# Cross attention: where SP issues the store of a batch's normalised rows

## What is computed

```python
def _L1_xattn_ref(q, k, v, gamma):              # q = x, k = v = ctx_2048: (8, 256, 512)
    qh = q.reshape(B, 8, 32, 512)               # 8 heads of 32 of the 256 rows
    ...
    qk = jnp.einsum('bhdq,bhdl->bhql', qh, kh) * scale
    sm = jax.nn.softmax(qk, axis=-1)            # over the 512 columns of the context
    ret = jnp.einsum('bhql,bhdl->bhdq', sm, vh)
    return gamma * ret.reshape(B, 256, 512)

x = _layernorm(x + _L1_attn_ref(x, ...))
x = _layernorm(x + _L1_xattn_ref(x, ctx_2048, ctx_2048, gamma))    # this stage
x = _layernorm(x + _L1_ffn_ref(x, ...))                            # experts
return x
```

## Time and profile before

| | us |
|---|---|
| median of 3 runs | 1998.21 |
| the runs | 2000.76, 1998.21, 1996.4 |
| the profiled execution | 2000.18 |
| its span, first to last instruction | 1998.4 |
| mean granted TensorE clock (share of full) | 0.965 |
| PE / DVE / ACT / POOL busy | 1812.1 / 1244.1 / 930.9 / 299.9 |

### The profile page before, as it was taken

One profiled execution on the slowest core, in us unless ns is written; L12 is line 12 of the kernel. 1 busy time (PEld: TensorE's weight loads), 2 busy tenths in 40 slices (PEclk: granted clock), 3 DMA queues, 4 the chain that ended last, 5 costly groups with the idle time before them and its releaser, 6 DMA issues. The chain is left out here.

```text
span 1998.4 us, 33002 instructions
## 1 busy us (share of the span) xinstructions
PE 1812.1 (91%) x12272; PEld 1488.5 (74%) x12272; DVE 1244.1 (62%) x2286; ACT 930.9 (47%) x2388; POOL 299.9 (15%) x377
## 2 busy tenths in 40 slices
PE   7999999999996999999999996799997698888985
PEld 6889999998984878888888885677775455555554
DVE  4654444444438655555554526788887588778866
ACT  2333333333334433333333213667667488887843
POOL 0000000000012111111111001333334212112012
PEclk9999999999998999999999997999997799999998
DMA  4310000000024221101110013001002576564612
GB/s 161 110 60 1 22 22 22 22 22 22 1 66 120 86 73 43 48 27 34 46 37 17 11 43 126 11 31 35 33 22 82 151 182 146 134 162 112 157 43 84
DMA packets 83581, 131.42 MB, mean 66 GB/s; under 512 B 9344, under 2 KB 25344, under 8 KB 83424
## 3 DMA queue, kind: packets, MB, share of 16 engines
q1 hardware_dynamic: 83424, 129.33, 22.7%
HBM read 75.21 MB, written 20.53 MB: 48 GB/s over the span
## 5 line engine op out<-in xcount | busy, mean ns | idle before, releaser
L2262 ACT ACTIVATE e_p<-e_s_ps,e_nb 128x512 f32<-128x512 f32 x256 | 175.6, 702 | 45.6 <-DVE e_nb L2326 43.5
L2326 DVE TENSOR_REDUCE e_nb<-e_s_ps 128x2 f32<-128x1024 f32 x128 | 155.8, 1217 | 50.6 <-PE e_s_ps L2421 49.6
L1703 ACT ACTIVATE p<-p,nb,rq 128x128 f32<-128x128 f32 (+1 forms) x256 | 136.9, 541 | 93.2 <-DVE nb L1804 93.2
L2431 PE MATMUL e_t_ps<-ident,e_p 128*128 128x128 f32 x1024 | 147.9, 284 | 22.0 <-DVE e_pT L2333 13.4
L2431 PEld LDWEIGHTS e_t_ps<-ident,e_p 128*128 128x128 f32 x1024 | 120.8, 146 | 59.2 <-issue 50.7
L887 PE MATMUL yp<-ccy,toep 128*128 128x288 f32 x600 | 158.9, 412 | 5.8 <-ACT ccy L869 4.0
L1224 DVE SCALAR_TENSOR_TENSOR hm<-gu_ps,us_col,sg 128x256 f32<-128x256 f32 x88 | 42.3, 480 | 177.7 <-ACT sg L1113 177.7
L80 PE MATMUL q_ps<-a_xt_hi,wq_hi 128*128 128x256 f32 x512 | 149.8, 293 | 0.0
L82 PE MATMUL q_ps<-a_xt_hi,wq_lo 128*128 128x256 f32 x512 | 145.0, 283 | 0.0
L472 ACT ACTIVATE ex<-ex 128x512 f32<-128x512 f32 x64 | 40.4, 632 | 223.7 <-DVE ex L565 223.7
L81 PE MATMUL q_ps<-a_xt_lo,wq_hi 128*128 128x256 f32 x512 | 144.6, 283 | 0.0
(11 more groups left out here) (339 smaller groups left out, 5150.0 us busy)
## 6 DMA issues: line engine op xcount, KB each, us to landing
x_after<-n_r SPq DMA_DIRECT2D x23, 512.0 KB, 3.1
toep<-padded_kernels SPq DMA_DIRECT2D x32, 256.0 KB, 3.6
qs<-e_xh SPq DMA_DIRECT2D x64, 128.0 KB, 2.5
qs<-e_xl SPq DMA_DIRECT2D x64, 128.0 KB, 2.6
ks<-e_ch SPq DMA_DIRECT2D x64, 128.0 KB, 2.6
ks<-e_cl SPq DMA_DIRECT2D x64, 128.0 KB, 2.6
x<-in_x SPq DMA_DIRECT2D x8, 512.0 KB, 4.1
a_x<-in_x SPq DMA_DIRECT2D x8, 512.0 KB, 4.2
```

What stands on the lines that cost most here:

```text
L1703: act.activation(p[n % 3][:, h, part[t]], p[n % 3][:, h, part[t]], ACT.Exp, bias=nb[i][:, t, h:h + 1], scale=rq[u][:, t:t + 1], accum_out= ...
L2262: act.activation(pr[i][:, a, :], s_ps[i][:, a, :], ACT.Exp, bias=nb[i][:, a:a + 1], accum_out=sums[t][:, j, q:q + 1]).then_inc(e_done, 1)
L2326: dve.tensor_reduce(nb[i][:], s_ps[i][:], AX.X, ALU.max, negate=True).then_inc(nb_done, 1)
L2431: last = pe.transpose(t_ps[a][:, k, :], pr[m % 2][:, a, k * P:(k + 1) * P], core.ident[:])
```

## The change

In SP's body the store of batch b - 1, with its wait for `y_done`, moves for 0 < b < 7 from the end of the body to just behind the stacking transfers. So it stands ahead of the wait for `c_turned`, of the loads of x and context b + 3 (batches 1 to 4; batches 5 and 6 have no loads), and of the residual's load. Batch 0 stores nothing, and in batch 7 the store stays behind the experts' loads. No instruction is added or removed, on SP or elsewhere.

```diff
--- before.py
+++ after.py
@@ -2177,6 +2177,8 @@
                 def body(b, u, more):
                     if not (ints(b) and b == B - 1):
                         stack(b + 1, 1 - u)
+                    if 0 < b < B - 1:
+                        norm.store(sp, b - 1)
                     if more:
                         sp.wait_ge(c_turned, 2 * b + 4)
                         load(b + 3, 1 - u)
@@ -2188,7 +2190,6 @@
                         for c in range(4):
                             sp.wait_ge(norm.stored, 16 * c + 16)
                             ex.load_x(sp, c)
-                    if not (ints(b) and b == 0):
                         norm.store(sp, b - 1)
                 for b in range(B):
                     body(b, b % 2, b < B - 3)
```

## The result

The changed kernel takes 1980.88 us (median of 6 runs, 1977.56 to 1984.26) against 1997.31 us (median of 6, 1991.12 to 2000.76) before: a ratio of 0.9916, 95% interval 0.9901 to 0.9931. Gains are given by the ratio from here on: 16.8 us less (13.8 to 19.8). In a second series it was 1978.08 (5 runs) against 1996.43 (9 runs), ratio 0.9911 (0.9897 to 0.9925), 17.8 us less (15.0 to 20.6). The changed kernel's profiled execution took 1980.6 us with a span of 1978.8. One far slower run of the kernel before, of 2092.49 us at a mean granted clock of 0.834, is counted in no ratio.

The account below looks back on a forecast made before the run. Late stores holding the residual add, and so TensorE, were taken to bound cross attention; 11.0 us direct plus 8.6 us of clock, 19.6 us off the median of 1998.21, gave 1978.6 us, range 1975 to 1989.

Parts of the forecast that it names:

- The bound: Cross attention, batches 0 to 7: a store of rows nobody reads there holds up the residual add, for which TensorE waits.
- Batch 6 as a control: Batch 6, whose add has no stall for its store, gives the period without the stall, 39.09 us at clock 1.00.
- The direct term: Batches 2 to 5: TensorE goes on 2.44 instead of 5.19 us after L2344, 2.75 us each, 11.0 us in all.
- POOL's hold: In the stalled batches the late add misses the gap, and POOL's second subtraction adds its own length to the stall.
- The clock's term: Batches 2 to 5: without the 3.18 us wait TensorE's clock stays up, 8.6 us in all, bounds 0 and 8.6.
- the sum: Whole gain forecast for batches 2 to 5, direct part and clock together: 19.6 us off.
- The rival of the direct part only: Batches 2 to 5: the clock falls for another reason, so only 11.0 us go: 1987.2 us; chance 12%.
- The rule of the Trainium skill: Half the time at a lowered clock is lost: about 11 us in four batches, whole gain 22 instead of 19.6.
- The new wait on SP: SP waits for `y_done` ahead of `c_turned`, with the loads behind it; L239 ends 4.45 us ahead of them: cost nothing.
- Batches 5 and 6: No loads there; the store moves ahead of the residual's load alone, first read in batch 7: gain nothing.
- The rival of no gain: The add misses POOL's gap anyway, or `y_done` comes no earlier than `c_turned`: 1998.2 us; chance 6%.
- The landing in the new place: Time the moved stores 0 to 3 take to land: taken at 3.5 us, between 2.8 and 9.1.

Follow-up runs that it names:

- the filling: On the kernel before, 16 small matmuls issued three times instead of once in step 2 of batches 2 to 5: 1993.55 us, ratio 0.9977.

## Why the prediction was right

*The bound.* Batch 6 as a control held: all of batches 2 to 5 came out at its 39.1 us, and the add, the gap and TensorE's restart match it to 0.01 us.

*The direct term*, 11.0 us, came as worked out (5.19 to 2.44 us after L2344). Its two parts were shown apart: with the late store kept and only POOL's hold taken away, the stall of batch 3 fell by 2 us.

*The clock's term*, 8.6 us, is real: keeping TensorE busy in the stall restored 36.66 us for 39.14. But it was mis-sized as a forecast for the median. In the profile that it was read from, three of four stalls cost 2.4 to 2.5 us of clock and one 1.2. In the six stalls of the runs with only batches 1 and 2, and only 5 and 6, moved, two cost over 2.2 and four 1.2 to 1.3 (periods of 44.1 to 44.2 and of 43.0 to 43.2, less 41.85, which is 39.10 and the direct 2.75). The mean of all ten is 1.8, so four stalls cost 7.3, and the sum would have been 18.3 us. It also fits the filling: 7.3, less the 1.0 us by which TensorE went on later there, is 6.3, inside the timed 2.0 to 7.2. What decides between the two prices of one and the same wait no run shows. The measured 16.8 and 17.8 us have intervals that hold both 18.3 and 19.6. The rival of the direct part only, 11.0 us, lies outside both intervals. That ordinary runs draw the smaller price more often is argued, not shown: they have no trace here. What is on record for them points that way: 41 timed runs of the kernel before had a mean granted clock of 0.966 to 0.972 over the whole program, and the profiled one 0.965. The stages that the change doesn't touch move the total by 1 to 2 us as well.

*The rule of the Trainium skill* ("TensorE: Matmul & The Clock Gate", "HAM oscillation") that half of the lowered time is lost would have given an estimated 22 us. In every stalled batch the traces show a smaller loss: for a mean of 0.96 over 43.2 us the rule gives an estimated 1.7, the traces 1.2 to 1.3. That the rest lies beside other engines' work, as the prediction took it, is not shown.

*The new wait on SP* cost nothing, and the loads could be held 4.8 us more for nothing. *Batches 5 and 6* gave nothing that a profile shows. The rival of no gain needed the add to miss POOL's gap; in the profile after it came through ahead of the second subtraction's end in every batch from 1 to 6. The landing in the new place, taken at 3.5 us between 2.8 and 9.1, was 2.7 to 3.6, 0.1 us below the lower bound, which cost the sum nothing.

## What to carry to other kernels

A store that nobody reads soon still has a reader of its buffer: look for who writes the buffer next, and issue the store as soon as its data stand, ahead of loads whose use is a whole batch away. Price such a stall by a neighbouring batch that doesn't have it, from restart to restart, since the wait itself was little more than half of its cost here. And before moving a transfer, look at what else holds the instruction that waits: one wait on POOL, which had time to spare, was worth 9 us with the late store left where it was.

## What the runs showed of the hardware

A wait of 3.18 us of TensorE cost 1.2 to 1.3 us of clock in five stalls and 2.3 to 2.5 in the other five. In this place waits of up to 2.13 us left the clock at 1.00, one of 2.51 did not (0.96). Repeated small matmuls in the wait kept it at 1.00 and paid for themselves (4.6 us less in the timed runs).

The issue of one and the same load by SP (the context's, 512 KB) took about 0.5 us mostly, but 0.86 to 1.74 us in 21 of 60 issues of the twelve profiles, and what stood behind it in the queue was issued later by as much. Its cause is open.

VectorE's add of two SBUF tensors, 0.69 us alone, never ended while a POOL subtraction that had begun before it was running: it ended 0.54 or 0.55 us behind it, 0.73 to 2.88 us after its start. Each time it was ready for the gap of 0.4 us between two subtractions it got through there. Where POOL's subtraction began second, behind the add by 0.13 us, it was the one that took longer (2.80 us for 2.34 to 2.40, batch 4 with the store behind both loads).
